# Own y and squares buffers for a batch's second half, squares summed over every fourth position, and a new order of all steps

## The reference, cut to what matters

```
qh = softmax over each head's 64 channels of (Wq @ layernorm(x)), times 1/8
kh = softmax over positions of (Wk @ ctx);   vh = Wv @ ctx
out = Wo @ (per head: (kh @ vh^T) applied to qh) + bo          # 128 x 1024
norm = max(sqrt(sum over the 128 channels of out * out), 1e-12)  # one number per position
x = x + tanh(g_xattn) * out / norm * g * sqrt(128)
h = layernorm(x)
gate, up = h @ deq(w_gate).T, h @ deq(w_up).T     # 2752 columns each
x = x + tanh(g_ffn) * ((gate * up) @ deq(w_down).T)
# deq(w) = round(clip(w / (mean|w| + eps), -1, 1)) * mean|w|: three values per weight
```

## Time and profile before

| | |
|---|---|
| median of the runs | 1391.26 us |
| the profiled execution, device time | 1387.74 us |
| its span, first to last instruction | 1385.9 us |
| TensorE busy | 1304.8 us (94%) |
| VectorE busy | 965.7 us (70%) |
| ScalarE, GpSimd busy | 624.6 us (45%), 565.4 us (41%) |
| mean granted clock of TensorE | 0.977 of full speed |
| read from HBM, written to it | 160.76 MB, 26.02 MB |

### The profile page before, as it was taken

One profiled execution on the slowest core, in us unless ns is written; L12 is line 12 of the kernel. 1 busy time (PEld: TensorE's weight loads), 2 busy tenths in 40 slices (PEclk: granted clock), 3 DMA queues, 4 the chain that ended last, 5 costly groups with the idle time before them and its releaser, 6 DMA issues. The chain is left out here.

```text
span 1385.9 us, 29984 instructions
## 1 busy us (share of the span) xinstructions
PE 1304.8 (94%) x12280; PEld 948.9 (68%) x12280; DVE 965.7 (70%) x1343; ACT 624.6 (45%) x879; POOL 565.4 (41%) x357
## 2 busy tenths in 40 slices
PE   5887498899999999999999999999999999999999
PEld 3554285665678657976588757976598757985994
DVE  5986677587888877788778776777568865842230
ACT  3888676564434534354335443454334443420220
POOL 0178732674455462554333632344234331331120
PEclk7998799999999999999999999999999999999999
DMA  9959799999475899787797777967798776657421
GB/s 355 390 199 309 221 298 280 213 224 187 110 163 162 175 203 245 196 179 164 188 206 189 163 177 176 234 155 164 141 232 199 175 166 146 160 140 182 142 89 53
DMA packets 410631, 268.43 MB, mean 194 GB/s; under 512 B 330432, under 2 KB 347200, under 8 KB 410496
## 3 DMA queue, kind: packets, MB, share of 16 engines
q1 hardware_dynamic: 403584, 241.36, 71.0%
q10 hardware_dynamic: 6912, 25.17, 5.7%
HBM read 160.76 MB, written 26.02 MB: 135 GB/s over the span
## 5 line engine op out<-in xcount | busy, mean ns | idle before, releaser
L1126 PE MATMUL ps<-w_dn,inter_buf 128*128 128x512 fp8e4 x1376 | 304.3, 379 | 1.4 <-issue 1.4
L1126 PEld LDWEIGHTS ps<-w_dn,inter_buf 128*128 128x128 f16 x1376 | 134.3, 99 | 156.7 <-issue 1.5
L1814 POOL TENSOR_TENSOR qs<-qs,q_stat 128x1024 f32<-128x1024 f32 x64 | 126.7, 1984 | 162.8 <-DVE q_stat L1623 162.4
L1042 PE MATMUL ps<-zT,w_gu 128*128 128x256 f16 x1664 | 190.1, 275 | 0.1
L1042 PEld LDWEIGHTS ps<-zT,w_gu 128*128 128x128 fp8e4 x1664 | 164.1, 99 | 25.6 <-issue 1.1
L1077 PE MATMUL ps<-w_gu 128*128 128x128 f16 x2880 | 173.4, 219 | 1.5 <-ACT w_gu L1138 0.8
L1077 PEld LDWEIGHTS ps<-w_gu 128*128 128x128 fp8e4 x2880 | 164.9, 98 | 4.0 <-issue 1.8
L1870 POOL TENSOR_TENSOR w_gu<-w_gu 128x512 f32<-128x512 f32 x60 | 82.2, 1371 | 176.2 <-DVE w_gu L1725 132.7
L1725 DVE SCALAR_TENSOR_TENSOR w_gu<-ps,w_gu 128x512 f32<-128x512 f32 x120 | 81.9, 687 | 92.4 <-PE ps L1077 91.6
L1077 PE MATMUL ps<-zT,w_gu 128*128 128x128 f16 x2176 | 132.6, 219 | 0.5 <-DMA w_gu<-forms 0.5
L1077 PEld LDWEIGHTS ps<-zT,w_gu 128*128 128x128 fp8e4 x2176 | 125.1, 98 | 2.4 <-DMA w_gu<-forms 0.7
(11 more groups left out here) (193 smaller groups left out, 2518.6 us busy)
## 6 DMA issues: line engine op xcount, KB each, us to landing
w_gu<-forms SPq DMA_DIRECT2D x158, 256.0 KB, 4.2
ct_raw<-forms SPq DMA_DIRECT2D x52, 256.0 KB, 4.2
w_dn<-in_down_w SPq DMA_DIRECT2D x19, 512.0 KB, 5.8
xb<-in_x ACTq DMA_DIRECT2D x16, 512.0 KB, 5.0
ysq<-r_dram SPq DMA_DIRECT2D x32, 256.0 KB, 4.2
x_dram<-xb SPq DMA_DIRECT2D x16, 512.0 KB, 3.9
fin<-x_dram SPq DMA_DIRECT2D x32, 256.0 KB, 3.6
out<-fin SPq DMA_DIRECT2D x32, 256.0 KB, 3.1
```

The lines of the kernel that those rows point to most:

```text
L1042: last = nc.tensor.matmul(ps[:, rest_bank(g, j), s * T:s * T + T], w_gu[:, w, k, :], zT[:, h, k, :], start=(k == 0 and h == 0), stop=(k == ...
L1126: mm = nc.tensor.matmul(ps[:, down_bank(g, k), :], inter_of(g, j, u % 2, b), w_dn[:, j, hf * 512:hf * 512 + 512], start=(u == 0), stop=(u ...
L1814: nc.gpsimd.tensor_tensor(v, v, q_stat[:, u % 2, 1, :].unsqueeze(2).broadcast_to([P, 2 * HEADS, DH]), ALU.mult).then_inc(q_prob, 1)
```

## The change

It has three parts.

1. **Buffers.** From batch 4 on, the second half of a batch has its y in `stage_c[:, 0, 0:512]` and its squares in `stage_c[:, 0, 512:1024]`. Its `yev` then needs the half before last to be done, not the last. The first `yev` that writes there waits until all 66 chunks are quantized. The semaphores of the store and the read back are split by halves.
2. **Positions.** `ss` takes every fourth position: matmul k has positions 4p+k as its stationary operand, read with a step of four float32 elements. What comes back from HBM is then in order, and `x2m` reads it without a step.
3. **Order.** All lists of `WHEN` have new numbers. No step moves to another engine, and no step is added or taken out.

```diff
+        def y_of(i, hf):
+            if hf == 0 or i < GB * PLAIN:
+                return y, sq
+            return stage_c[:, 0, 0:512], stage_c[:, 0, 512:1024]
...
             def put_r(i, hf):
                 wait(sp, rs_ready, 2 * i + hf + 1)
-                ... .then_inc(r_stored, 16)
+                ... .then_inc(r_stored[hf], 16)
             def get_r(i, hf):
-                wait(sp, r_stored, 16 * (2 * i + hf + 1))
-                sp.dma_start(sq, ...).then_inc(r_in, 16)
+                wait(sp, r_stored[hf], 16 * (i + 1))
+                sp.dma_start(y_of(i, hf)[1], ...).then_inc(r_in[hf], 16)
...
             def ss(i, hf):
                 wait(pe, y_ready, 2 * i + hf + 1)
                 wait_banks(out_free)
+                v = y_of(i, hf)[1].rearrange("c (p k) -> c k p", k=4)
                 for k in range(4):
-                    last = nc.tensor.matmul(ps[:, OUT, k:k + 1], sq[:, k * P:k * P + P], ones, start=True, stop=True)
+                    last = nc.tensor.matmul(ps[:, OUT, k:k + 1], v[:, k, :], ones, start=True, stop=True)
...
             def yev(i, hf):
                 wait(act, out_ready, 2 * i + hf + 1)
-                wait(act, x2_ready, 2 * i + hf)
-                wait(act, ss_ready, 2 * i + hf)
+                before = 2 * i + hf - (1 if 2 * i + hf > 2 * GB * PLAIN else 0)
+                wait(act, x2_ready, before)
+                wait(act, ss_ready, before)
+                if i == GB * PLAIN and hf == 1:
+                    act.wait_ge(wq_done, len(QUANT_OF))
+                v, v2 = y_of(i, hf)
...
             def x2m(i, hf):
-                wait(dve, r_in, 16 * (2 * i + hf + 1))
+                wait(dve, r_in[hf], 16 * (i + 1))
...
-                v = y.rearrange("c (k p) -> c k p", k=4)
-                nc.vector.scalar_tensor_tensor(out=v, in0=sq.rearrange("c (p k) -> c k p", k=4), ..., in1=v, ...)
+                v, r = y_of(i, hf)
+                nc.vector.scalar_tensor_tensor(out=v, in0=r, ..., in1=v, ...)
...
             def rs(i, hf):
                 wait(pool, ss_guarded, 2 * i + hf + 1)
-                wait(pool, r_stored, 16 * (2 * i + hf - 1))
+                wait(pool, r_stored[hf], 16 * i)
```

More of the change, by code:

```diff
@@ L93 @@
 WHEN = {
[L94 to L98, removed]
@@ L110 @@
[L110 to L115, removed]
@@ L124 @@
[L124 to L140, removed]
[3 rows of a table removed]
@@ new lines @@
+    "kexp": [34, 35, 92, 94, 189, 227, 238, 260, 294, 381, 416, 424, 465, 647, 648, 697, 754, 793, 887, 939, 1061,
+        1074, 1128, 1154, 1166, 1277, 1278, 1351, 1352, 1454, 1474, 1532, 1721, 1739, 1777, 1799, 1929, 1953, 1958,
+        1992, 2095, 2160, 2204, 2241, 2366, 2367, 2393, 2408, 2542, 2596, 2649, 2654, 2816, 2818, 2832, 2839, 2971,
+        3004, 3057, 3070, 3207, 3228, 3233, 3234],
+    "ktr": [66, 84, 108, 109, 183, 215, 256, 276],
+    "k_f": [85, 100, 129, 142, 178, 216, 251, 270],
@@ new lines @@
+    "kf_hi": [344, 407, 442, 469, 570, 650, 701, 770, 819, 858, 947, 995, 1072, 1097, 1136, 1235, 1244, 1300, 1329,
+        1384, 1410, 1456, 1569, 1606, 1754, 1773, 1796, 1802, 1936, 1966, 1986, 2000, 2111, 2175, 2206, 2242, 2372,
+        2389, 2417, 2464, 2554, 2611, 2655, 2678, 2817, 2829, 2850, 2886, 2975, 3039, 3083, 3099, 3219, 3232, 3266,
+        3273],
+    "kf_lo": [387, 431, 483, 501, 581, 663, 725, 757, 830, 907, 958, 985, 1084, 1098, 1137, 1230, 1259, 1309, 1347,
+        1415, 1460, 1507, 1576, 1607, 1756, 1778, 1791, 1832, 1959, 1983, 2014, 2036, 2144, 2195, 2213, 2248, 2361,
+        2416, 2426, 2453, 2594, 2636, 2672, 2702, 2795, 2805, 2858, 2907, 2979, 3055, 3095, 3113, 3220, 3245, 3246,
+        3274],
@@ new lines @@
+    "krec": [155, 278, 449, 739, 981, 1161, 1365, 1608, 1805, 2059, 2290, 2423, 2715, 2854, 3068, 3257],
+    "cc_hi": [146, 302, 560, 845, 1003, 1281, 1448, 1640, 1864, 2063, 2305, 2497, 2709, 2902, 3151, 3327],
+    "cc_lo": [156, 288, 576, 846, 1012, 1282, 1481, 1638, 1861, 2081, 2301, 2519, 2725, 2934, 3146, 3333],
+    "mprod": [141, 323, 563, 861, 1022, 1306, 1477, 1662, 1890, 2080, 2332, 2512, 2740, 2958, 3163, 3328],
+    "mev": [167, 301, 606, 855, 1030, 1291, 1500, 1659, 1870, 2096, 2302, 2533, 2736, 2937, 3147, 3353],
@@ new lines @@
+    "tr": [99, 138, 213, 214, 291, 293, 373, 374],
+    "e_f": [101, 149, 221, 228, 287, 321, 395, 396],
+    "qf_hi": [426, 542, 588, 666, 721, 827, 904, 957, 968, 999, 1000, 1088, 1116, 1167, 1240, 1342, 1372, 1408,
+        1479, 1547, 1596, 1672, 1715, 1763, 1787, 1889, 1904, 1947, 1993, 2070, 2139, 2189, 2209, 2251, 2318, 2386,
+        2460, 2505, 2536, 2616, 2660, 2707, 2789, 2815, 2872, 2942, 3003, 3032, 3081, 3093, 3206, 3226, 3289, 3343,
+        3384, 3414],
+    "qf_lo": [470, 547, 591, 692, 758, 835, 896, 921, 962, 998, 1011, 1089, 1111, 1179, 1248, 1349, 1386, 1452,
+        1517, 1567, 1585, 1689, 1726, 1765, 1808, 1901, 1938, 1965, 2040, 2100, 2142, 2186, 2216, 2249, 2331, 2394,
+        2449, 2528, 2586, 2613, 2689, 2717, 2769, 2794, 2903, 2949, 3001, 3019, 3094, 3110, 3195, 3229, 3302, 3361,
+        3383, 3416],
@@ new lines @@
+    "turn_q": [491, 550, 676, 715, 804, 844, 884, 946, 980, 1026, 1059, 1076, 1124, 1194, 1279, 1374, 1407, 1493,
+        1510, 1537, 1566, 1703, 1766, 1794, 1878, 1896, 1933, 1948, 2060, 2061, 2146, 2179, 2239, 2304, 2350, 2374,
+        2481, 2491, 2562, 2598, 2638, 2699, 2770, 2771, 2884, 2908, 3016, 3021, 3074, 3109, 3198, 3287, 3320, 3367,
+        3418, 3432],
+    "outp": [158, 159, 160, 161, 252, 253, 267, 269, 325, 326, 338, 345, 377, 378, 379, 382, 608, 610, 611, 634,
[6 rows of a table added]
+    "yev": [202, 268, 368, 406, 636, 750, 934, 982, 1092, 1138, 1322, 1376, 1525, 1625, 1755, 1792, 1930, 1971,
[3 rows of a table added]
@@ new lines @@
+    "store_form": [339, 423, 429, 1120, 1121, 1135, 1150, 1151, 1152, 1153, 1195, 1196, 1226, 1227, 1228, 1229,
+        1237, 1238, 1262, 1263, 1289, 1301, 1324, 1331, 1332, 1377, 1379, 1434, 1435, 1450, 1451, 1485, 1489, 1495,
+        1496],
+    "form": [320, 1113, 1114, 1129, 1157, 1172, 1185, 1186, 1188, 1273, 1307, 1308, 1333, 1339, 1356, 1378, 1458,
+        1464, 1487, 1488],
+    "load_form": [1502, 1503, 1504, 1521, 1522, 1523, 1526, 1527, 1549, 1551, 1552, 1553, 1554, 1559, 1560, 1643,
[11 rows of a table added]
@@ new lines @@
+    "l_hi": [68, 73, 74],
+    "l_lo": [72, 79, 296],
+    "wpart": [223, 224, 674],
+    "wtotal": [243, 244, 699],
+    "wscale": [230, 231, 703],
+    "consts": [5],
+    "prod": [33],
+    "gains": [67],
+    "wload": [12, 13, 14, 15, 16, 17, 18, 19, 20, 21, 22, 23, 24, 25, 26, 27, 28, 29, 30, 31, 32, 38, 39, 40, 41,
[5 rows of a table added]
+    "wsum": [48, 46, 47, 50, 49, 51, 52, 53, 75, 76, 77, 90, 107, 117, 121, 122, 131, 130, 132, 133, 134, 135, 157,
+        136, 163, 165, 164, 168, 171, 182, 192, 193, 204, 206, 203, 205, 208, 209, 207, 212, 239, 240, 241, 242,
+        545, 551, 552, 546, 554, 555, 553, 592, 599, 603, 624, 625, 618, 628, 629, 630, 631, 632, 652, 651, 653,
+        654],
@@ L339 @@
+    "put_r": [144, 290, 372, 439, 691, 785, 888, 951, 1079, 1156, 1341, 1398, 1619, 1622, 1770, 1803, 1969, 1970,
+        2221, 2252, 2363, 2420, 2565, 2637, 2821, 2825, 3079, 3080, 3281, 3325, 3437, 3482],
+    "get_r": [172, 305, 383, 453, 714, 803, 941, 1008, 1081, 1191, 1392, 1409, 1623, 1644, 1790, 1841, 1984, 1985,
+        2261, 2262, 2373, 2438, 2591, 2656, 2834, 2835, 3087, 3090, 3334, 3352, 3467, 3505],
 }
@@ L543, in gated_attention_ffn @@
         ss_ready, ss_guarded, rs_ready = sem("ss_ready"), sem("ss_guarded"), sem("rs_ready")
-        r_stored, r_in = sem("r_stored"), sem("r_in")
+        r_stored, r_in = ([sem(f"{n}{h}") for h in range(2)] for n in ("r_stored", "r_in"))
         y_scaled, x2_ready, x2_stored = sem("y_scaled"), sem("x2_ready"), sem("x2_stored")
```

212 lines of the change are left out of this document (90 added, 122 removed), and 205 rows, old and new, of the table WHEN.

## The result

| | before | after |
|---|---|---|
| median of 4 runs each, side by side | 1389.72 us | 1410.05 us |
| lowest to highest | 1383.13 to 1392.24 | 1405.37 to 1416.10 |
| profiled execution, device time / span | 1387.74 / 1385.9 us | 1411.08 / 1409.0 us |
| TensorE busy / idle in the span | 1304.8 / 81.1 us | 1337.3 / 71.7 us |
| of this idle time, before / after 315 us | 70.8 / 10.4 us | 55.8 / 15.9 us |

The kernel became slower: ratio 1.0156, 95% interval 1.0102 to 1.021. The forecast was 1385 us, which counts as no change; the time is that of rival 1, 1410 us. TensorE has 32.5 us more to do and stands still for 9.4 us less; the sum, 23.1 us, is the whole difference of the spans.

What follows compares the result with a forecast made beforehand. TensorE bounds the kernel after 315 us (1060.5 of 1071 us busy), so gains lie in the first 280 us. Terms -0.4 -2.3 +0 -2 -2 +2.8 -1 = -4.9 us from 1387.7 give 1382.8, as a median 1385; range 1371 to 1415.

Steps and rivals of the forecast that it cites:

- rival 1: L1017, ss: each stepped weight load takes twice its 98 ns, +25 us, giving 1410 us; chance 0.34.
- ss with a step of four: TensorE's 256 ss passes: the step was taken to cost 0 us, with bounds 0 and +48 us.
- The slack argument: TensorE's ss load: one-byte pairs come every 56 ns, so the 98 ns float32 load has slack for a step.
- VectorE's difference: ss load priced by x2m's extra time with a step, 0.88 ns per element: +29 us over 256 loads.
- x2m without a step: VectorE's x2m: 1144 ns falls to 691; 14.5 us spared, worth -2.3 us in the early loop, 0 after 315 us.
- Buffers: Second halves from batch 4 on: waits for squares after 315 us total 0.6 us; gain taken as -0.4 us.
- The new order, early: Norm's loop in the early batches: reordered steps priced one by one, -2.2 us for its four items, +-8 allowed.
- four items: Early loop: outp ahead -2 us, z(0) ahead -2, weight loads between put_r and get_r +2.8, transpose gone there -1.
- Rival 2: Batch 1's loop, put_r to get_r: the store of r no longer stuck, 8.7 us more gained, 1376 us; chance 0.15.
- Rival 3: Early loop: another store, for instance (1,1)'s, gets stuck, +8.7 us, 1394 us, no gain; chance 0.13.
- What would show it: Listed signs: ss 0.79 or 1.6 us, x2m near 0.69, TensorE 99% busy after 315 us, early idle 60 to 68.
- the prediction's second sign of being wrong: After 315 us: a TensorE wait over 3 us, where no row of before has one.

Runs made afterwards that it cites:

- experiment 2: Kernel before with only the positions changed (step of four in ss, plain x2m), old order and buffers: 1411.95 us against 1387.10, ratio 1.0166.
- experiment 7: Kernel before, old order and buffers, with ScalarE writing squares in place and x2m reading without a step: 1390.13 us against 1388.22, ratio 1.0031.
- Experiment 3: Kernel before with the second buffers and split semaphores alone, old order and positions: 1390.58 us against 1387.10, ratio 1.0020.
- experiment 12: Experiment 8's order with the small weights' scales issued before the third weight sum on VectorE: 1384.11 us against the kernel before's 1388.55, ratio 0.9972.
- experiment 8: New order only for steps with old numbers under 900, new buffers, old positions: 1383.18 us against the kernel before's 1388.22, ratio 0.9973.
- experiment 1: Changed kernel with its positions undone (new order and buffers, ss over neighbours, x2m stepped): 1390.33 us against the kernel before's 1387.10, ratio 1.0026.
- experiment 4: Changed kernel, but ScalarE writes squares in place so ss reads neighbours and x2m stays plain: 1388.18 us, ratio 1.0006 to the kernel before.

## Why the prediction was wrong, step by step

**The step that failed: "ss with a step of four", "I take 0".** It was read from the right rows: nothing hides `ss`, the price was bounded by 0 and 48 us, and its likeliest values there were 0 and 25. The choice between them went by the nearest row of the same engine, on the argument that a float32 load has slack, since a one-byte pair comes every 56 ns and this one every 98. The runs show no such slack at full clock: the load's own median goes from 192 to 329 ns, and a pass grows by 107 ns (118 ns with both at full clock), that is 0.83 to 0.92 ns for each of 128 elements. VectorE's difference, 0.88 ns in the prediction and the base of its +29 us, lies between. Measured are +27.3 us in the group, 27.7 us of busy time in the old order (experiment 2), and +24.9 us of time there. The slack argument compared the pace of one kind of load with that of another, and said nothing of what sets the float32 one. VectorE's row, where the same step was in the trace with its price, was the better guide. The prediction's 98 ns is the pace of the passes, not the length of a load, which was 192 ns.

**That the time is rival 1's almost to the microsecond is in part luck.** Rival 1 took twice the 98 ns, 25 us, on top of a gain of 5 us that did not come: the kernel without the step took 1390.33 us, not 1385. In this order the step itself cost 21.6 us of span and not 25. Its place was right and its size near, its sum is two misses that nearly cancel.

The loads took 196 ns with a step of 8 bytes, 329 with 16 and 334 with 32. The Trainium skill's "Advanced Engine Details and Errata", SBUF Cachelines, wants two hits on a line of 16 bytes; by that rule the first has them and the others don't, and the traces agree. With the time by columns alone, of the Trainium skill's "TensorE: Matmul & The Clock Gate", LDWEIGHTS, the traces don't agree: the same 128 columns took 192 or 329 ns.

**x2m without a step: right in kind.** 1144 ns became 748, not 691; VectorE is spared 32 x 0.396 = 12.7 us. The 2.3 us forecast in the loop were never measured by themselves: experiment 7 shows no gain at the end, but there a longer square stands against it.

**Buffers: right.** Experiment 3; 0.4 us is too little to be told.

**The new order, early: no gain came out, where -2.2 was forecast for its four items.** The four items looked at a few places in the loop. The loop as a whole begins late in the new order: the first `ss` at 73.23 instead of 72.09, the next at 103.40 instead of 95.98, batch 1's first at 134.83 instead of 125.60, and the first feed-forward matmul at 177.92 instead of 172.39. The prediction followed only the steps near the norm. A wait for a scale that lies before them was 1.9 us long, ending at 20.0 us, and is now 7.9 us long and ends at 26.7; but that is not what puts the loop off, for the first `ss` is only 1.1 us late, and experiment 12, which moves this scale, gains nothing on experiment 8 that can be told. Another 6.3 us are lost between batch 0's two halves and 1.8 up to batch 1's first; which steps there cost them was not tested one by one. Still TensorE was busy for 15.0 us more by 315 us (259.24 against 244.24; 254.36 in experiment 1, the rest goes with the step): the new order fills the stretch from 140 to 280 us, where its granted clock from 210 us on is 0.98 instead of 0.93. Then it has less at hand: idle time behind 315 us is 10.4 us before, 15.9 after, 21.0 in experiment 1.

**Rival 2's place was true, its gain was not.** The read back of (1,0) follows by 2.5 us, as was said would show it. But the rival priced the wait as if the turn started when it did before. A wait that goes is worth its length only if the thing behind it isn't put off by other moves. Rival 3 did not come: the read back of (1,1) follows its store by 3.1 us.

**What would show it: what came true.** `ss` at 1.65 to 2.01 us, where 1.6 was the sign of rival 1. A wait over 3 us after 315 us (3.2, for the issue of L1050), the prediction's second sign of being wrong; experiment 1 has it too (3.8 us) and can't be told from the kernel before, so it was no sign of this slowdown. Idle time in the first 280 us: 280 - (43.93 + 55.31 + 57.03 + 68.50) = 55.2 us, under the forecast 60 to 68. x2m near 0.69 us: 0.748. TensorE 99% busy after 315 us: 1078.1 of 1094. Its waits for the squares there: 0.6 us.

**What stays open.** Which later steps give the new order's 10 us back: the waits of experiment 1 behind 315 us are small and spread over several lines (3.8 us, 3.2 in 4, 3.0 in 2, 2.1, 1.3, 1.0), and no kernel moved them one by one. Nor was a stepped moving operand tried, nor a stepped load of two-byte elements.

## What to carry to other kernels

Where an access gets a step, price it from the nearest row with the same step, on whatever engine, before the nearest row of the same engine without it; put the step on the engine that has room (the move to ScalarE cost 0.47 us an instruction, nothing that could be told in experiment 4 and 0.3% in experiment 7), or keep it at 8 bytes. An order of steps is worth what TensorE's idle time says over the whole run, with its early and late parts shown apart; a stall at one place says little. A part of an order can be worth more than all of it: here 0.3% for its early steps, nothing that can be told for all. Where the bound engine's clock is not the same everywhere, compare a row only with rows at its own clock: the same plain load took 192 or 333 ns.

## What the runs showed of the hardware

- A float32 load of 128 columns into TensorE at full clock: 192 ns contiguous, 196 with a step of 8 bytes, 329 with 16, 334 with 32. At a granted clock of 0.50: 333 ns contiguous, 329 with 16 bytes.
- VectorE's x2m, 128x512 float32: 1144 ns with one operand read with a step of 16 bytes, 748 without.
- ScalarE, 128x512 float32 from PSUM: 770 ns, 1240 with the results written 512 bytes apart.
- A store of 2 KB lands after 2.6 us in 16-byte pieces, 3.9 in 8-byte pieces.
